# Skip term on VectorE, output projection by halves, MLP two rows sooner, VectorE unrolled, B row first

## The reference

```
# layer 0: norm, then a forward and a backward mamba on the 1024 positions
u, z = split(xz); u = silu(conv1d(u))
dt, Bm, Cm = split(u @ x_proj_w.T)
delta = softplus(dt @ dt_proj_w.T + dt_proj_b)
h = exp(delta * A) * h + delta * u * Bm          # 16 states n, a scan over positions
y = sum_n(h * Cm) + u * D_param                  # the skip term, one for each direction
out = (y * silu(z)) @ out_proj_w.T
x = x + res_scale * (scale_mod * (fwd + bwd) + sigmoid(dwconv(x_norm)) * x_norm)
# layer 1, on tokens
t = t + softmax_causal(q k / 8) v @ Wo + bo      # 6 heads of 64, on layernorm(t)
t = t + gelu(layernorm(t) @ w_fc.T) @ w_proj.T
```

## Time and profile before

| what | value |
| --- | --- |
| median of three runs | 4229.28 us (4217.98 to 4236.39) |
| the profiled execution | 4223.39 us, span 4221.6 us |
| VectorE (DVE) busy | 3587.6 us, 85% |
| TensorE (PE) busy | 3382.0 us, 80% |
| GpSimd (POOL) busy | 2733.4 us, 65% |
| ScalarE (ACT) busy | 2560.3 us, 61% |
| data moved by DMA | 785.11 MB, mean 186 GB/s |

### The profile page before, as it was taken

How to read it: one execution, slowest core, us unless ns; L and a number is a source line. 1 busy time by engine, 2 the same in 40 slices (tenths; PEclk the granted TensorE clock), 3 DMA queues, 4 the chain that set the end, 5 groups by cost and what they waited for, 6 DMA issues and landing times.

```text
span 4221.6 us, 40649 instructions
## 1 busy us (share of the span) xinstructions
PE 3382.0 (80%) x11610; PEld 1701.1 (40%) x11626; DVE 3587.6 (85%) x2721; ACT 2560.3 (61%) x3547; POOL 2733.4 (65%) x1692
## 2 busy tenths in 40 slices
PE   6503398978898798978889788988989789976997
PEld 2201145623364234732356233742356233641472
DVE  4999898998899998998989988999989998898121
ACT  3533557766675656756676666757667576765362
POOL 2888676676766767676766767667766777676000
PEclk9756699988999899988999899988999889997998
DMA  3999798887978889787978879888988889788000
GB/s 81 232 229 239 189 225 185 208 201 191 216 187 204 208 196 211 182 208 181 238 180 220 190 193 221 189 196 193 222 190 195 202 200 219 178 208 207 6 7 15
DMA packets 224024, 785.11 MB, mean 186 GB/s; under 512 B 25292, under 2 KB 40958, under 8 KB 223518
## 3 DMA queue, kind: packets, MB, share of 16 engines
q0 software_dynamic: 117504, 427.87, 52.4%
q1 hardware_dynamic: 106270, 354.32, 25.6%
HBM read 339.60 MB, written 39.85 MB: 90 GB/s over the span
## 4 chain that ended last, share of the span: by engine, by line
PE 35%; DVE 25%; issue 13%; DMA 11%; POOL 8%; ACT 7%; DVEq 0%; SPq 0%; ACTq 0%; POOLq 0%
DVE pB L1198 17%; PE pW L668 9%; PE pW L585 9%; DMA y<-hb 7%; POOL hb L1375 6%; PE pW L473 4%; DMA y<-area 3%; PE pW L516 3%; PE pW L601 2%; ACT pt L1002 2%; PE pW L735 2%; DVE hb L1207 2%; PE pW L550 2%; POOL y L1386 1%; DVE pB L1163 1%
## 5 line engine op out<-in xcount | busy, mean ns | idle before, releaser
L1198 DVE TENSOR_TENSOR_SCAN pB<-pB,hb 128x1024 f32<-128x1024 f32 x768 | 1757.0, 2288 | 40.2 <-POOL hb L1375 20.1
L1386 POOL DMA_DIRECT2D y<-hb x768 | 747.3, 973 | 736.6 <-DVE hb L1207 627.6
L1375 POOL TENSOR_TENSOR hb<-du_f,b_row 128x1024 f32<-128x1024 f32 x384 | 1036.8, 2710 | 131.9 <-DMA b_row<-bc_rows 108.3
L1375 POOL TENSOR_TENSOR hb<-uc_b,b_row 128x1024 f32<-128x1024 f32 x384 | 995.3, 2593 | 61.8 <-DMA y<-hb 60.2
L1207 DVE TENSOR_TENSOR hb<-pB,c_row 128x1024 f32<-128x1024 f32 x768 | 940.4, 1224 | 44.3
L821 ACT ACTIVATE pB<-delta,vec 128x1024 f32<-128x1024 f32 x384 | 428.8, 1117 | 383.7 <-DVE hb L1207 383.3
L821 ACT ACTIVATE pB<-xres,vec 128x1024 f32<-128x1024 f32 x384 | 429.1, 1119 | 325.7 <-DVE hb L1207 325.0
L668 PE MATMUL pW<-area,pt 128*128 128x64 f32 x3456 | 432.6, 279 | 20.0 <-ACT pt L1002 12.4
L668 PEld LDWEIGHTS pW<-area,pt 128*128 128x128 f32 x3456 | 405.0, 193 | 69.8 <-ACT pt L1002 59.7
L1242 DVE TENSOR_REDUCE stat<-pW 128x1 f32<-128x640 f32 (+7 forms) x361 | 258.7, 753 | 163.4 <-PE pW L588 163.4
L492 PE MATMUL pW<-area,xn_area 128*128 128x512 f32 x576 | 265.4, 616 | 41.5 <-DVE area L1285 27.0
(11 more groups left out here) (172 smaller groups left out, 4890.7 us busy)
## 6 DMA issues: line engine op xcount, KB each, us to landing
y<-hb POOLq DMA_DIRECT2D x768, 512.0 KB, 7.2
b_row<-bc_rows SPq DMA_DIRECT2D x256, 512.0 KB, 5.8
c_row<-bc_rows SPq DMA_DIRECT2D x256, 512.0 KB, 5.5
du_f<-in_x SPq DMA_DIRECT2D x8, 1536.0 KB, 13.6
kept_residual<-in_x SPq DMA_DIRECT2D x8, 1536.0 KB, 13.0
y<-area POOLq DMA_DIRECT2D x24, 512.0 KB, 8.0
xres<-kept_residual SPq DMA_DIRECT2D x8, 1536.0 KB, 10.5
out_x<-xa SPq DMA_DIRECT2D x8, 1536.0 KB, 6.8
```

What stands on the lines that cost most here:

```text
L1198: dve.tensor_tensor_scan(flow(d, buf), flow(d, buf), flow(d, hb[r % NHB][:, :]), 0.0, ALU.mult, ALU.add).then_inc(scan_done, 1)
L1375: pool.tensor_tensor(hb[r % NHB][:, :], du[d][:, k, :], b_row[g % 2][:, :], ALU.mult)\
L1386: pool.dma_start(y[:, k, :], hb[r % NHB][:, :], accum_op=ALU.add).then_inc(y_in[k], 16)
```

## The change

Six edits in one:

- **Skip term.** `skip(b, 1, k)`, `sum_skip` and the extra count of `y_in` go. In rows 21, 19 and 20 (k = 0, 1, 2) `output_row` multiplies in PSUM, then a second VectorE instruction adds u * D and writes `hb`.
- **Output projection by halves.** `ctx_t`, `wo` and `wo_add` take all three channel blocks of the first half of the tokens, then of the second; `ctx_t` one row sooner, `wo` and `wo_add` two rows, three `wo_add` a row.
- **MLP** and its norm two rows sooner (the second `mlp_add` in row 93 in place of 95), with `next_in` moved too; some step and projection rows shift by one.
- **VectorE's program** is written out for all iterations.
- **B row first.** `narrow_copies` copies `bc_raw` before `dtr`; the store waits for the first copy, `step_size` for the second.
- **kept adds.** GpSimd issues the three accumulations into `kept` behind the inputs of rows 0, 1 and 2 and not ahead of row 0.

```diff
-YIN = 16 * (2 * NS + 1)
+YIN = 16 * 2 * NS
-SKIP = (24, 27, 30)
+SKIP = (21, 19, 20)
-BEHIND = ([("step_silu", 0, 17), ("step_x", 0, 19)] + [("step_skip", k, 18 + k) for k in range(KT)]
-          + [(kind, k, (22, 26, 29)[k] + i) for k in range(KT)
+BEHIND = ([("step_silu", 0, 17), ("step_x", 0, 19)] + []
+          + [(kind, k, (22, 25, 28)[k] + i) for k in range(KT)
-S0, S1 = 33, 62
-PROJ = (15, 16, 17, 18, 19, 21, 22, 22, 23, 24, 24, 25, 26, 26, 27, 28, 29, 30, 31, 31)
+S0, S1 = 33, 61
+PROJ = (15, 16, 17, 18, 19, 20, 21, 22, 23, 23, 24, 25, 26, 26, 27, 28, 29, 30, 31, 31)
-    + [("ctx_t", t, S1 + t // 3) for t in range(6)] + [("wo", t, S1 + 2 + t // 3) for t in range(6)]
-    + [("wo_add", t, S1 + 3 + t // 2) for t in range(6)]
+    + [("ctx_t", t, S1 + t // 3) for t in range(6)] + [("wo", t, S1 + 1 + t // 3) for t in range(6)]
+    + [("wo_add", t, S1 + 2 + t // 3) for t in range(6)]
-    + norm(1, S1 + 5, S1 + 7, S1 + 8, S1 + 10, S1 + 11)
+    + norm(1, S1 + 4, S1 + 6, S1 + 7, S1 + 9, S1 + 10)
-    + [("mlp_in", 0, S1 + 12), ("mlp_cast", 0, S1 + 13), ("mlp_split", 0, S1 + 14)] + mlp(0, S1 + 14) + mlp(1, S1 + 24)
+    + [("mlp_in", 0, S1 + 11), ("mlp_cast", 0, S1 + 12), ("mlp_split", 0, S1 + 13)] + mlp(0, S1 + 13) + mlp(1, S1 + 23)
...
-                sp.wait_ge(xd_evac, at(4, b, 2 * d + 2))          # store_rows
+                sp.wait_ge(xd_evac, at(4, b, 2 * d + 1))
-                pe.wait_ge(xd_evac, at(4, b, (1, 1, 2, 4, 4, 4)[g]))   # step_size
+                pe.wait_ge(xd_evac, at(4, b, 2 * d + 2))
+                act.copy(bc_raw[d], bank[0:32, :]).then_inc(xd_evac, 1)
                 act.copy(dtr[d][0:RANK, :], bank[32:56, :]).then_inc(xd_evac, 1)
-                act.copy(bc_raw[d], bank[0:32, :]).then_inc(xd_evac, 1)
...
-                    pe.wait_ge(ct_evac, at(6, a, 6))              # wo
-                    if n >= 4:
+                    if n < 4:
+                        pe.wait_ge(ct_evac, at(6, a, n + 3))
+                    else:
                         pe.wait_ge(wo_add, at(6, a, n - 3))
...
-                    if n >= 14 and n % 2 == 0 and not alone(b):   # ScalarE, proj
-                        k = n // 2 - 7
-                        act.wait_ge(y_in[k], at(YIN, b, 16 * ((SKIP[k] - LAG - k) // KT + 2)))
...
+                if r == SKIP[k]:                                  # output_row
+                    dve.tensor_tensor(pBC[r % 2][:, :], pBC[r % 2][:, :], c_row[g % 2][:, :], ALU.mult)\
+                       .then_inc(skip_step, 1)
+                    dve.wait_ge(uc1_ready, at(3, b, 3))
+                    dve.wait_ge(skip_step, at(KT, b, sorted(SKIP).index(r) + 1))
+                    dve.scalar_tensor_tensor(out=hb[r % NHB][:, :], in0=uc[1][:, k, :], scalar=vec[:, k, V_D:V_D + 1],
+                                             in1=pBC[r % 2][:, :], op0=ALU.mult, op1=ALU.add).then_inc(m2_done, 1)
...
-            samples(dve, iteration)
+            for b in range(NB + 1):
+                iteration(b, b < NB, b > 0, b < NB - 1)
...
+            def keep_local(b, k):
+
+                pool.wait_ge(loc_ready, at(KT, b, k + 1))
+                pool.dma_start(kept[b][128 * k:128 * k + 128, :], gate[k], accum_op=ALU.add).then_inc(kept_add[k], 16)
...
-                    for k in range(KT):
-                        pool.wait_ge(loc_ready, at(3, b, k + 1))
-                        pool.dma_start(kept[b][128 * k:128 * k + 128, :], gate[k], accum_op=ALU.add)\
-                            .then_inc(kept_add[k], 16)
                     for r in range(ROWS):
                         input_row(b, r)
+                        if r < KT:
+                            keep_local(b, (1, 0, 2)[r])
                         if r >= LAG:
                             sum_row(b, r - LAG)
-                        if r in SKIP:
-                            sum_skip(b, SKIP.index(r))
```

More of the change, by code:

```diff
@@ L95 @@
     norm(0, 7, 9, 10, 12, 13) + [("proj", t, PROJ[t]) for t in range(NPJ)] + attention()
-    + [("ctx_t", t, S1 + t // 3) for t in range(6)] + [("wo", t, S1 + 2 + t // 3) for t in range(6)]
-    + [("wo_add", t, S1 + 3 + t // 2) for t in range(6)]
+    + [("ctx_t", t, S1 + t // 3) for t in range(6)] + [("wo", t, S1 + 1 + t // 3) for t in range(6)]
+    + [("wo_add", t, S1 + 2 + t // 3) for t in range(6)]
     + [("next_square", 0, S1 + 4), ("next_mean", 0, S1 + 4), ("next_rstd", 0, S1 + 5), ("next_norm", 0, S1 + 6)]
-    + norm(1, S1 + 5, S1 + 7, S1 + 8, S1 + 10, S1 + 11)
-    + [("next_in", t, S1 + (7, 10, 13)[t // 2]) for t in range(6)] + [("next_up", t, S1 + (8, 11, 14)[t // 2]) for t in range(6)]
-    + [("mlp_in", 0, S1 + 12), ("mlp_cast", 0, S1 + 13), ("mlp_split", 0, S1 + 14)] + mlp(0, S1 + 14) + mlp(1, S1 + 24), key=lambda x: x[2])
+    + norm(1, S1 + 4, S1 + 6, S1 + 7, S1 + 9, S1 + 10)
+    + [("next_in", t, S1 + (7, 9, 11)[t // 2]) for t in range(6)] + [("next_up", t, S1 + (8, 10, 12)[t // 2]) for t in range(6)]
+    + [("mlp_in", 0, S1 + 11), ("mlp_cast", 0, S1 + 12), ("mlp_split", 0, S1 + 13)] + mlp(0, S1 + 13) + mlp(1, S1 + 23), key=lambda x: x[2])
 SLOTS = [[(kind, n) for kind, n, row in STEPS + FINISH + PLAN + BEHIND if row == r] for r in range(ROWS)]
@@ L186, in hybrid_block @@
         uc = [uc_f, uc_b]
-        skip_row = [area1[:, k * L:(k + 1) * L] for k in range(KT)]
         du = [du_f, uc_b]
@@ L319, in landed @@
         def landed(r):
-            return 16 * (r // KT + 1 + (r > SKIP[r % KT] - LAG))
+            return 16 * (r // KT + 1)
         def flow(d, ap):
@@ L744, in item @@
                 elif kind == "next_mean":
-                    pe.wait_ge(wo_add, at(6, b - 1, 4))
+                    pe.wait_ge(wo_add, at(6, b - 1, 6))
                     pe.wait_ge(delta_ready, at(6, b + 1, 0))
@@ L887, in tap_row_of, with skip @@
                                        scale=w).then_inc(tap_ready, 1)
[L889 to L899, removed]
+            def skip(b, k):
+                act.wait_ge(uc_ready, at(6, b, 2 * k + 2))
+                act.wait_ge(yz_ready, at(3, b, 0))
+                act.activation(y[:, k, :], uc[0][:, k, :], ACT.Identity, scale=vec[:, k, V_D:V_D + 1])\
+                   .then_inc(yd_ready, 1)
             def copy_u(b, t):
@@ L929, in item @@
                 if kind == "step_y" and not early:
-                    skip(b, 0, n)
+                    skip(b, n)
                 elif kind == "step_z" and not early:
@@ L938, in item @@
                     act.preload_act_table_set(LOG_EXP)
-                elif kind == "step_skip" and not early:
-                    skip(b, 1, n)
                 elif kind == "step_bc" and early:
@@ L1077, in iteration @@
                     for k in range(2):
-                        skip(b, 0, k)
+                        skip(b, k)
                     for r, d, n, k in rows():
@@ L1206, in output_row @@
                 dve.wait_ge(scan_done, at(ROWS, b, r + 1))
-                dve.tensor_tensor(hb[r % NHB][:, :], pBC[r % 2][:, :], c_row[g % 2][:, :], ALU.mult)\
-                   .then_inc(m2_done, 1)
+                if r == SKIP[k]:
[5 more added lines that the diff above has]
+                                             in1=pBC[r % 2][:, :], op0=ALU.mult, op1=ALU.add).then_inc(m2_done, 1)
+                else:
+                    dve.tensor_tensor(hb[r % NHB][:, :], pBC[r % 2][:, :], c_row[g % 2][:, :], ALU.mult)\
+                       .then_inc(m2_done, 1)
             def item(kind, n, b, early):
@@ L1254, in item @@
                 elif kind == "wo_add" and not early:
-                    t, m, c = n, n // 2, n % 2
+                    t, m, c = n, n % KT, n // KT
                     toks = slice(c * HALF, (c + 1) * HALF)
                     dve.wait_ge(wo_ready, at(6, a, t + 1))
-                    dve.scalar_tensor_tensor(out=xa[:, m, toks], in0=pW[:, t % 4, :], scalar=vec[:, m, V_BO:V_BO + 1],
+                    dve.scalar_tensor_tensor(out=xa[:, m, toks], in0=out_bank(t), scalar=vec[:, m, V_BO:V_BO + 1],
                                              in1=xa[:, m, toks], op0=ALU.add, op1=ALU.add).then_inc(wo_add, 1)
@@ L1386, in sum_row @@
                 pool.dma_start(y[:, k, :], hb[r % NHB][:, :], accum_op=ALU.add).then_inc(y_in[k], 16)
-            def sum_skip(b, k):
-                pool.wait_ge(yd_ready, at(6, b, 4 + k))
-                pool.wait_ge(y_in[k], at(YIN, b, 16 * ((SKIP[k] - LAG - k) // KT + 1)))
-                pool.dma_start(y[:, k, :], skip_row[k], accum_op=ALU.add).then_inc(y_in[k], 16)
             def iteration(b, layer0, layer1, more):
```

13 lines of the change are left out of this document (7 added, 6 removed).

## The result

The changed kernel takes 4320.9 us in the median of four runs (4317.7 to 4326.1); the kernel before, in four runs beside them, 4225.9 (4218.0 to 4236.4). The ratio is 1.0224 with a 95% interval of 1.0198 to 1.0251: slower by about 95 us, where 40 were forecast and 4300 was the end of the range.

What follows compares the result with a forecast made beforehand. VectorE was taken to bound the kernel; turns 16 + 6.7 + 0.9, rows 17 to 34 -5, output projection +15 and tail +6 made +40 on 4229.3, 4269, given as 4265 us; range 4203 to 4300.

Steps and rivals of the forecast that it cites:

- What bounds the kernel: Whole kernel: VectorE is busiest, rows follow in order, so every VectorE wait or added instruction costs its duration.
- MLP two rows sooner: Turn between images: transfers issued before the last y accumulations delay them; +16 us at five turns, +6.7 at the sixth.
- I take E + 10.5: Turn between images: the last y accumulation lands 10.5 us after the end of row 95's product.
- E: Time mark at each turn between images: the end of row 95's product on VectorE.
- the prediction's own formula: Turn length: 3.95 wait and add, 10.5 landing, 38.2 to the scan, 0.9 B row: 53.6 us against 50.4.
- The lower case: Turn between images: warm x projection and a landing at E + 5.8 give 46.3 us, -4.1.
- The equal half: DMA engines at the turn: accumulations get half, landing at E + 7.6; six turns cost 7 us less than with E + 8.8.
- Output projection by halves: Rows 63 and 64: VectorE waits 5.8 us for wo, the wait before next_norm goes; +15 us over seven images.
- Second skip term: Rows 17 to 34: 4.1 us spent, 4.4 back an image from shorter soft_sum waits; -5 us in all.
- VectorE unrolled, B row first, kept adds: Turn and first rows: unrolling 0 with bound -14.5 us, B row +0.9, kept adds nothing.
- The tail: After image 7: the gated product waits for the last y accumulation, landing at about E + 9.5; +6 us.
- much slower: Rival for the whole kernel: landing at E + 12.5 or later, wo at half clock; about +70 us, 4300; 12%.

Runs made afterwards that it cites:

- the three mends: Changed kernel with three transfers held until the last y accumulations landed, next_in 0 and 1 ahead of ln_var in row 68, and later wo_add rows: 4223.4 us.
- b_unroll: Kernel before with VectorE's program unrolled alone: 4225.4 us, ratio 1.0008.
- a_swap: Changed kernel with next_in 0 and 1 put ahead of ln_var within row 68: 4299.6 us, ratio 1.0185.
- a_hold: Changed kernel with the store of xa and the transfers of xres and kept held until row 95's product is done: 4309.4 us, ratio 1.0204.
- a_land: Changed kernel with the store of xa and the transfers of xres and kept held until the last y accumulations landed: 4266.3 us, ratio 1.0104.
- b_skip: Kernel before with the second skip term by VectorE alone, with its rows for proj and softplus: 4229.3 us, ratio 1.0015.
- a_plan_back: Kernel before with skip term by VectorE, B row first, kept adds moved and VectorE unrolled; MLP and output projection as before: 4233.1 us, ratio 1.0019.
- b_halves: Kernel before with the output projection by halves alone, the MLP where it was: 4250.3 us, ratio 1.0051.

## Why the prediction was wrong, step by step

**What bounds the kernel** held in the main: the three mends took waits from VectorE, and the time fell by 95 us. But "every wait of VectorE is time of the kernel" was too strong. b_unroll took 14.5 us of idle from it, and nothing came off the time, because later waits grew.

**MLP two rows sooner: the mechanism was right, the landing was too small.** The transfers are issued where I said, `silu_u` 0 waits for the accumulation, the x projection is slow, `mlp_add` keeps its wait. The step that failed is "I take E + 10.5". The six landings lie at E + 13.3 to E + 14.5, beyond even the upper bound of 12.5 from the earlier trace rows. Put 13.6, that of image 3, into the prediction's own formula: 3.95 + 13.6 + 38.2 + 0.9 = 56.7, and the turn of image 3 is 52.9 + 1.93 + 1.75 = 56.6, which is +6.2. Over the five turns it is +33 and not +16, and +11 at the last one and not +6.7.

I reasoned from the first turn's share of 45% for accumulations, with only two behind the loads. But the two accumulations, 5.4 us of work, took from E - 3.2 to E + 13.6: a share of 32%, and 29.3 of 86.4 by the queue table. I had written that the added store "may push it". The changed kernel's own chain says that the store matters less than the copy into kept. Its first turn (E = 472.69) has xres and kept ahead and no store, and its end (E = 3983.00) has the store and xres and no kept:

```profile
472.99 12.88 DMA y<-hb
```

```profile
3983.30 8.77 DMA y<-hb
```

That is E + 13.2 without the store, and E + 9.1 without kept. In a_swap it is 12.5 and 11.0, with 14.0 to 15.7 for all three. But in a_hold, where the transfers go out beside the accumulation, the end without kept lands as late as the turns (10.8 from the issue). No run varied one transfer alone, so this is a reading and not a proof.

The lower case was mis-sized too. In a_land the landing is at E + 4.8 and the x projection takes 5.36, for which the formula gives 4.8 + 35.6 + 0.9 = 41.3 (35.6 is 38.2 less the 2.6 that the faster projection saves); the turn is 44.4. There the chain runs through VectorE's own taps, the last of which ends at E + 23.7, and the prediction had no such path.

The Trainium skill (DMA: Bandwidth & Descriptors, "Queues, rings and completion order") has the DMA engines take their queues in turn. It doesn't say that the shares are equal. The equal half that I made of it gave a landing at E + 7.6, and the trace doesn't bear that half out, with E + 13.3 and more.

**What was missing altogether: the wait of row 71.** I priced the parts that the diff moves against VectorE and SyncE, and not the order that two entries get on TensorE when they fall into one row. `norm(1, ...)` moved by two rows and `next_in` 0 and 1 by one. That is 3.8 to 4.1 us at six images, 24 us; the runs give 16 to 24. The prediction had nothing for it. It is as large an error as the landing, with which the six turns were forecast at 23 us and measured at 44, and a list of TensorE's order in rows 66 to 72, before and after, would have shown it.

**Output projection by halves: +15 forecast, about 20 measured.** The waits are 3.9 to 5.2 an image in three or four places (5.8 in four forecast), and the 2.7 before `next_norm` went as forecast. I had booked those 2.7 as a full gain. But two thirds of it came back (9.4 of 14.3 over the whole run), because one of the norm's three instructions then lasts 3.36 in place of 1.22, beside GpSimd's product.

**Second skip term: -5 forecast, +6 measured.** The first `soft_sum` waits 1.6 to 2.3 (1.85 forecast) and the third 2.2 to 3.4 (1.5). The second (1.8 forecast) waits 1.6 or 2.1 where TensorE's clock is at its high level in the later value projections, and 3.7 to 5.1 where it is low. Together they are 7.6 to 9.5 in an image of b_skip, where 5.1 was forecast, so the 4.4 that was to pay for the added instructions mostly did not come.

**VectorE unrolled, B row first, kept adds: 0, +0.9 and 0.** The sums held. The unrolled program alone is within 0.2% of no change, and a_plan_back less b_skip, which is the three together, is 0.04%; B row and kept adds were not run alone. But the zero of the unrolled program was partly luck. I had said that what the gap gives is waited for right behind the taps. About half of the 14.5 goes there; the rest goes in row 24, at the first `soft_sum`, which is 3.1 longer at five images because the value projections run at the 1.2 GHz level.

**The tail** held: +6 forecast. The last y accumulation lands at E + 9.1 (9.5 forecast), and the output projection starts at E + 10.4 (3993.37 - 3983.00), where 10.7 was forecast. With the 3.6 of `mlp_add` and its wait, that is 6.9 later than the old E + 7.0.

```profile
3983.30 0.86 POOL L1391 DMA_DIRECT2D y<-hb  x1 [2.60 <-DVE hb L1206]
...
3993.37 6.99 PE L473 MATMUL pW<-zs,w_qp 128*128 128x512 f32 x11 [19.09 <-DVE zs L1172]
```

**The sum again, with what was measured:** turns 33 + 11, row 71 24, `wo` 20, skip 6, tail 6: 100, against 96.6. Against the forecast the landing makes 21 of the difference, row 71 24, the skip term 11 and `wo` 5. Of the rivals "much slower" was the nearest, with a landing at E + 12.5 or later, and it had 12%. Its 4300 also lacked row 71.

What stays open: why b_halves, by the medians, is 29 us above the kernel before and by the ratio 22; which of the three transfers delays the landing; and what decides the level of TensorE's clock ahead of the first and the second `soft_sum`.

## What to carry to other kernels

When work is moved sooner, list what its completion releases. Here an add that went two rows ahead let three 1.5 MB transfers loose in front of the one small accumulation that the next stage waits for, and a wait on that accumulation's landing gave 51 us back. When entries of a hand-written plan fall into the same row, write down each engine's new order and look for one that waits ahead of one that is ready. Price a gap that closes only after naming the waits that come next, and not only the nearest: here neither the loop's gap of 14.5 us nor the skip term's slack was worth anything.

## What the runs showed of the hardware

An accumulating DMA of 512 KB lands in 4.5 us with no big transfer about (a_land), in 10.0 to 10.9 with three that are issued beside it (a_hold), and in 13.0 to 14.2 with the three issued 6 to 7 us ahead (the changed kernel; up to 15.4 in a_swap). I had expected 12.2 to be the worst.

The same 18 value projection matmuls take TensorE 6.07 us with a granted clock near full and 8.1 to 8.4 with 0.50, the 1.2 GHz level, and a wait of VectorE two engines further on then comes in two sizes, 4.2 or 7.4 us.

VectorE's norm instructions, with two inputs in SBUF, last 1.22 us alone. In the changed kernel the second of image 4 starts during GpSimd's product:

```profile
2359.34 1.22 DVE L1284 SCALAR_TENSOR_TENSOR area<-du_f,vec,prob 128x1024 f32<-128x1024 f32 x1
...
2360.47 3.36 DVE L1284 SCALAR_TENSOR_TENSOR area<-du_f,vec,prob 128x1024 f32<-128x1024 f32 x1
```

```profile
2359.78 2.96 POOL L1380 TENSOR_TENSOR hb<-uc_b,b_row 128x1024 f32<-128x1024 f32 x1
```

It lasts 3.36 and ends at 2363.83, 1.09 after GpSimd's product ends (2362.74), as if it had waited for that and then run. The Trainium skill (SBUF — State Buffer, "SBUF: two separate sides") says that the port pair which VectorE and GpSimd share is an exclusive lock, held for the whole instruction, also for a VectorE operation with two inputs in SBUF; the trace agrees, with these three lines. GpSimd's spans are rough in the profile, so the 1.09 is too. The scans and their products, which read PSUM, keep 2.29 and 1.22 beside the same GpSimd product.
